# Masked attention: score products in three half banks used in turn, new engine orders, and a later start of the last stage

## The reference, cut to what matters

```
x = x + cross_attention(layernorm(x), ctx)              # 16 heads of 16, with biases
x = x + two_of_eight_experts(layernorm(x))
q, k, v = layernorm(x) Wq, ctx Wk, ctx Wv                # shared 16x16 matrices per head
energy  = where(mask == 0, -1e20, q k^T)                 # the masked attention
x = x + softmax(energy / sqrt(256)) v Wo + bo
x = x + spikes(square(relu(layernorm(x) W_fc)) W_proj)   # the last stage
```

## Time and profile before

| | |
|---|---|
| median of three executions | 3887.06 us (3885.37 to 3891.0) |
| the profiled execution | 3889.76 us, of which the span of the trace is 3888.0 us |
| TensorE busy | 3699.7 us (95%) |
| VectorE busy | 3091.1 us (80%) |
| ScalarE busy | 2208.8 us (57%) |
| GpSimd busy | 2208.9 us (57%) |
| mean granted TensorE clock | 0.979 |

### The profile page before, as it was taken

The page is one execution under the profiler, slowest core; times in us unless marked ns, Lnnn a source line. Parts: engine busy times, 40 slices in busy tenths (PEclk is TensorE's granted clock), DMA queues, the critical chain, the costliest instruction groups (busy, mean ns, idle before and its releaser), DMA issues. The chain is left out here.

```text
span 3888.0 us, 134428 instructions
## 1 busy us (share of the span) xinstructions
PE 3699.7 (95%) x47408; PEld 2875.9 (74%) x47408; DVE 3091.1 (80%) x5266; ACT 2208.8 (57%) x4529; POOL 2208.9 (57%) x3316
## 2 busy tenths in 40 slices
PE   5999999994899999999999996899999989999999
PEld 4777777772677777777777775566666658888888
DVE  4888888886777777777777775799889877777777
ACT  3777777775444444444444442577767764555554
POOL 5666666663354533333333334366656667887777
PEclk9999999997899999999999998899999999999999
DMA  4677777765333322222222223699999962333332
GB/s 123 187 210 206 211 213 219 215 201 160 99 81 80 81 66 74 65 74 65 67 71 65 74 62 87 157 211 212 219 209 209 213 151 80 79 75 76 79 75 72
DMA packets 834241, 502.59 MB, mean 129 GB/s; under 512 B 262037, under 2 KB 824408, under 8 KB 833480
## 3 DMA queue, kind: packets, MB, share of 16 engines
q1 hardware_dynamic: 832680, 493.49, 50.3%
q0 software_dynamic: 928, 0.49, 0.1%
HBM read 251.27 MB, written 214.96 MB: 120 GB/s over the span
## 5 line engine op out<-in xcount | busy, mean ns | idle before, releaser
L1506 ACT ACTIVATE all_region<-phase_loop_hid,phase_b1T 128x128 f32<-128x128 f32 x2048 | 586.1, 368 | 728.0 <-PE phase_loop_hid L193 693.5
L191 PE MATMUL phase_loop_hid<-phase_loop_moe_h,phase_w_hi 128*128 128x128 f16 x4096 | 728.1, 220 | 0.1
L193 PE MATMUL phase_loop_hid<-phase_loop_moe_h,phase_w_lo 128*128 128x128 f16 x4096 | 726.4, 219 | 0.0
L192 PE MATMUL phase_loop_hid<-phase_loop_moe_h,phase_w_hi 128*128 128x128 f16 x4096 | 726.4, 219 | 0.0
L1112 DVE TENSOR_REDUCE phase_loop_mx<-phase_loop_score 128x8 f32<-128x1024 f32 x512 | 625.8, 1222 | 100.6 <-PE phase_loop_score L875 94.8
L1472 PE MATMUL phase_loop_moe_y<-phase_w,all_region 128*128 x2048 | 693.6, 379 | 0.3
L1030 ACT ACTIVATE phase_loop_pt<-phase_loop_scoreT 128x1024 f32<-128x1024 f32 x448 | 458.6, 1024 | 271.5 <-PE phase_loop_scoreT L909 269.2
L1474 PE MATMUL phase_loop_moe_y<-phase_w,all_region 128*128 x2048 | 558.2, 273 | 0.0
L1524 DVE TENSOR_SCALAR all_region<-all_region 128x512 f16<-128x512 f32 x512 | 257.6, 503 | 248.6 <-PE phase_loop_moe_y L1474 192.8
L191 PEld LDWEIGHTS phase_loop_hid<-phase_loop_moe_h,phase_w_hi 128*128 x4096 | 400.6, 98 | 66.5 <-issue 0.4
L1527 DVE SCALAR_TENSOR_TENSOR all_region<-all_region 128x512 f16<-128x512 f32 x512 | 410.1, 801 | 17.6
(11 more groups left out here) (276 smaller groups left out, 9846.6 us busy)
## 6 DMA issues: line engine op xcount, KB each, us to landing
qk_scratch<-phase_loop_qk SPq DMA_DIRECT2D x192, 256.0 KB, 3.5
phase_loop_qS<-qk_scratch SPq DMA_DIRECT2D x768, 64.0 KB, 3.2
phase_loop_cin<-in_ctx SPq DMA_DIRECT2D x128, 256.0 KB, 4.6
x_scratch<-phase_loop_x SPq DMA_DIRECT2D x128, 256.0 KB, 3.1
h_scratch<-phase_loop_hr SPq DMA_DIRECT2D x128, 256.0 KB, 3.8
phase_loop_kS<-qk_scratch SPq DMA_DIRECT2D x384, 64.0 KB, 2.4
ks_scratch<-ct_scratch SPq DMA_DIRECT2D x384, 64.0 KB, 2.4
phase_loop_kS<-ks_scratch SPq DMA_DIRECT2D x128, 192.0 KB, 3.9
```

The source lines that it names most:

```text
L191: eng.matmul(out, l_hi, r_hi, start=start, stop=False)
L192: eng.matmul(out, l_hi, r_lo, start=False, stop=False)
L193: return eng.matmul(out, l_lo, r_hi, start=False, stop=stop)
L1506: i = act.activation(hf[n % NF][:, j, :], hid(u, n)[:, j * S:(j + 1) * S], ACT.Gelu, bias=w["b1"][:, bass.ds(e * HB + (4 * half + j), 1)], ...
```

## The change

Only phase 3 differs.

- The scores go into three half banks in turn: the two of `score` and `ring0`. The eight halves of a unit (n = 0 to 3, hh = 0 and 1) are numbered on through all units, and half number i is in bank i mod 3. The 8 products of `score(n)` are the same; each now writes to the bank of its half.
- `mask_score` handles one half: one matmul of 512 columns, which waits for the half three places before to be read.
- `row_max(n)`, one reduction of 1024 columns, becomes two, `row_max_half(n, 0)` and `row_max_half(n, 1)`, of 512 columns each. The semaphore `s_mx` counts to 8 per unit.
- `o` changes to the ring bank of `t_max`, `q` and `y0`; `t_y` and `y1` share the other one.
- The task lists of all five engines get a new order and, in part, new lags. Nothing else is added or left out.
- `NEXT_START` goes from 5 to 9 (VectorE 6 to 10): the tasks of the last stage join the lists four steps later.

```diff
-NEXT_DEPTH, NEXT_START = 5, dict(zip(("sync", "tensor", "scalar", "gpsimd", "vector"), (5, 5, 5, 5, 6)))
+NEXT_DEPTH, NEXT_START = 5, dict(zip(("sync", "tensor", "scalar", "gpsimd", "vector"), (9, 9, 9, 9, 10)))
...
-        s_s, s_mx, s_st, s_e, s_av = (g(n, NP) for n in "s_s s_mx s_st s_e s_av".split())
+        s_s, s_st, s_e, s_av = (g(n, NP) for n in "s_s s_st s_e s_av".split())
+        s_mx = g("s_mx", NP if first else 2 * NP)
...
-            plan = [(8, "t_y"), (4, "t_max"), (1, "q"), (7, "y1"), (6, "y0"), (8, "o")]
-            shared = ((), ("t_max", "q", "o"), ("t_y", "y1", "y0"))
+            plan = [(9, "o"), (8, "t_y"), (4, "t_max"), (1, "q"), (7, "y1"), (6, "y0")]
+            shared = ((), ("o", "t_max", "q", "y0"), ("t_y", "y1"))
...
+        score3 = half_banks(score_bank) + [ring3[0][:, :]]
+
+        def score_half(u, n, hh):
+
+            return score3[(2 * (NP * u.no + n) + hh) % 3]
...
-                    tasks = [(5, load_c), (1, load_xT), (5, store_max), (3, stack_q), (11, store_x1), (12, store_h),
-                             (2, store_q), (8, load_r), (5, place_max), (2, stack_k)]
+                    tasks = [(5, place_max), (0, load_xT), (2, stack_k), (4, store_max), (2, stack_q), (4, load_c),
+                             (10, store_x1), (11, store_h), (7, load_r), (1, store_q)]
...
-                    tasks = [(11, rows1), (4, maxima), (5, ctx_as_v), (6, cut(p, 3)), (9, rstd1)]
+                    tasks = [(5, ctx_as_v), (9, rstd1), (3, maxima), (10, rows1), (5, cut(p, 3))]
...
-                                m = pe.matmul(score_bank[:, half(hh, j)], qS[u.slot4][rows, b, at], kS[u.slot4][rows, b, at],
+                                to = score_bank[:, half(hh, j)] if first else score_half(u, n, hh)[:, j * S:(j + 1) * S]
+                                m = pe.matmul(to, qS[u.slot4][rows, b, at], kS[u.slot4][rows, b, at],
...
-                def mask_score(n):
+                def mask_score(n, hh):
 
                     def go(u):
-                        s_mx.wait(pe, u, n)
-                        for hh in range(2):
-                            pe.matmul(score_bank[:, hh * 512:(hh + 1) * 512], c["identb"][:, :], w["mask"][:, :], start=True,
-                                      stop=False, skip_group_check=True)
+                        s_mx.wait(pe, u, 2 * n + hh - 2)
+                        pe.matmul(score_half(u, n, hh), c["identb"][:, :], w["mask"][:, :], start=True, stop=False,
+                                  skip_group_check=True)
...
-                    tasks = [(6, av(0)), (3, score(0)), (8, make["t_y"]), (5, mask_score_t(0)), (4, make["t_max"]),
-                             (5, score_t(0)), (3, mask_score(1)), (6, av(1)), (3, score(1)), (5, score_t(1)),
-                             (1, make["q"]), (7, make["y1"]), (3, mask_score(2)), (5, mask_score_t(2)), (3, score(2)),
-                             (6, av(2)), (5, score_t(2)), (6, av(3)), (3, mask_score(3)), (6, make["y0"]),
-                             (3, score(3)), (5, score_t(3)), (8, make["o"]), (2, mask_score(0))]
+                    tasks = [(4, score(3)), (6, score_t(3)), (3, mask_score(0, 0)), (9, make["o"]),
+                             (3, mask_score(0, 1)), (8, make["t_y"]), (6, av(0)), (3, score(0)), (5, mask_score_t(0)),
+                             (3, mask_score(1, 0)), (4, make["t_max"]), (6, av(1)), (5, score_t(0)),
+                             (3, mask_score(1, 1)), (1, make["q"]), (3, score(1)), (5, score_t(1)),
+                             (3, mask_score(2, 0)), (7, make["y1"]), (6, av(2)), (3, mask_score(2, 1)),
+                             (5, mask_score_t(2)), (3, score(2)), (5, score_t(2)), (3, mask_score(3, 0)),
+                             (6, make["y0"]), (3, mask_score(3, 1)), (6, av(3))]
...
-                    tasks = [(5, copy_max), (6, expo(0)), (6, expo(1)), (2, hi_q), (7, copy_y(0)), (6, expo(2)),
-                             (7, copy_y(1)), (10, norm1), (6, expo(3)), (6, expo_under(3)), (8, hi_y)]
+                    tasks = [(8, hi_y), (10, norm1), (4, copy_max), (5, expo(0)), (6, copy_y(0)), (1, hi_q),
+                             (5, expo(1)), (5, expo(2)), (6, copy_y(1)), (5, expo(3)), (5, expo_under(3))]
...
+                def row_max_half(n, hh):
+                    a, g4 = n // 2, n % 2
+
+                    def go(u):
+                        s_s.wait(v, u, n + 1)
+                        if n == 0 and hh == 0:
+                            s_m3.wait(v, u.back(2))
+                        to = mx[u.slot][:, a, :].rearrange("p (h g j) -> p h g j", h=2, g=2)[:, hh, g4, :]
+                        v.tensor_reduce(to, score_half(u, n, hh).rearrange("p (j n) -> p j n", j=CH), AX.X,
+                                        ALU.max).then_inc(s_mx.sem, 1)
+                    return go
...
-                    tasks = [(8, norm_y(0)), (10, add_x), (4, row_max(0)), (10, norm1_stats), (9, lo_y),
-                             (4, row_max(1)), (8, norm_y(1)), (2, lo_q), (4, row_max(2)), (6, cut(v, 1)),
-                             (4, row_max(3))]
+                    tasks = [(4, row_max_half(0, 0)), (9, lo_y), (4, row_max_half(0, 1)), (10, norm1_stats),
+                             (4, row_max_half(1, 0)), (2, lo_q), (4, row_max_half(1, 1)), (8, norm_y(1)),
+                             (4, row_max_half(2, 0)), (4, row_max_half(2, 1)), (7, norm_y(0)),
+                             (4, row_max_half(3, 0)), (4, row_max_half(3, 1)), (6, cut(v, 1)), (9, add_x)]
```

## The result

The changed kernel takes **3932.84 us** (median of 4 executions, 3927.45 to 3934.9) against 3888.39 us for the kernel before in the same session. The ratio is **1.0112, 95% interval 1.0095 to 1.013**: slower by 44 us, outside my range (3873 to 3904). The profiled execution has a span of 3932.0 us, also 44.0 more than the 3888.0 of before.

What follows compares the result with a forecast made beforehand. TensorE was taken as really full at 11.36 us a unit in the steady masked attention. Terms 1 + 4 - 6 + 5.1 = +4.1 us gave 3893.9 on the profiled execution, 3891.2 us as median, range 3873 to 3904.

Steps and rivals of the forecast that it cites:

- loop C: From score(3) through its halves and GpSimd's maxima to t_max: possible at 4.3 us, its place at 4.43, so it fits.
- The new order of waits: Walk through one steady unit's three tight loops: all fit by about 0.1 us; +1 us taken for 57 units.
- TensorE's floor: TensorE's work per steady unit is unchanged by the change and stays 11.36 us.
- VectorE and the halves: Eight half reductions cost VectorE +0.3 us a unit, 10.7 in all, hidden under 11.36; taken as 0.
- second rival: VectorE becomes the bound in the steady units, slower: 3902 to 3914 us, chance 0.12.
- the point of 0.70 us a half: Length of a half reduction from which VectorE's load would decide the steady unit; at 0.75 us, 23 us more.
- The DMA queue: In four steps with large transfers TensorE waits 2.7 us for place_max's rows, plus lower clock: 15.6 for 11.6, +4 us.
- first rival: The waits for place_max's rows vanish as transfers land sooner: 3873.2 us, chance 0.2.
- Fill: Start of phase 3: three banks shorten the mask and reduction loop, t_max comes earlier in the first units; -6 us.
- Drain and later start: End of phase 3: first up product 12.8 us later after a 10.0 us gap, 7.7 regained behind it; +5.1 us.
- steps 66 to 68: Steps of the drain after t_y of unit 58: 28.0 us in the new lists, about as before.
- third rival: The ends cost more, by large transfers holding TensorE or low clock through the drain: +12, 3899 us, chance 0.18.

Runs made afterwards that it cites:

- e1: The changed kernel with VectorE's cut of quarter 1 handling one head's 128 columns in place of all eight: 3909.69 us, ratio 1.0049.
- f6: The kernel before with each row_max split into two half reductions, two banks and all orders as they were: 3885.89 us, ratio 0.9998.
- e3: The changed kernel with t_max behind av(1) in TensorE's list in place of ahead of it: 3933.33 us, ratio 1.0108.
- f4: The kernel before with place_max alone moved, to behind stack_q in the DMA queue's list: 3899.79 us, ratio 1.0025.
- e4: The changed kernel with the last stage beginning two steps earlier (NEXT_START 7 in place of 9): 3925.24 us, ratio 1.0085.
- g2: The kernel before with cut(1) behind row_max(3) in VectorE's list, so that it runs beside GpSimd's maxima: 3916.44 us, ratio 1.0077.
- f1: The changed kernel with place_max behind stack_q in the DMA queue's list, 2.3 us earlier and ahead of the large transfer: 3952.23 us, ratio 1.0163.

## Why the prediction was wrong

**The failed step is loop C of "The new order of waits".** It took the maxima's 2.34 us from a unit in which they run alone, and put t_max possible at 4.3 us against its place at 4.43: "All fit, by about 0.1 us". The new list puts the cut directly behind the last half, beside them. That is 1.06 - 0.29 = 0.77 us more; less the 0.13 of room it is 0.64, and e1 measured 0.66. The rest of the loop came as I had walked it. My +1 us for the loops became +30: the new wait of 0.66 us a unit, less 0.12 that the new list saves (below), 57 times. The page "SBUF — State Buffer" of the Trainium skill (section "Who interferes with whom") has the rule: a VectorE instruction with two inputs in SBUF contends with a GpSimd instruction that reads SBUF, and of the modes in which VectorE takes the whole pair of shared ports it says that whoever issues first has the pair for the whole instruction and the other blocks fully. The traces here agree with the first for this `tensor_tensor`, and nearly with the second: where the cut starts first, L757 ends with it, within 0.15 us; where L444 starts first with 0.61 us still to go, the cut is 0.47 us longer. I had read the earlier trace rows without that question. The kernel before even showed it: its cut takes 1.69 us in the steady part, where GpSimd's L444 (1.16 us) has started first, and 1.22 in its drain, where L444 has not; and in that drain a GpSimd operation of 0.23 us takes 0.80 beside the cut (timelines of GpSimd and VectorE, kernel before):

```profile
3162.52 0.23 POOL L423 TENSOR_SCALAR phase_loop_ln1b_nm<-phase_loop_ln1b_mv 128x2 f32<-128x2 f32 x1
...
3182.83 0.80 POOL L423 TENSOR_SCALAR phase_loop_ln1b_nm<-phase_loop_ln1b_mv 128x2 f32<-128x2 f32 x1
...
3182.32 1.22 DVE L585 TENSOR_TENSOR phase_loop_pt<-phase_loop_pt,all_keep_min 128x1024 f32<-128x1024 f32 x1
```

An earlier start alone does not hold the other up: L412 (`tensor_tensor` of 128x2, 0.73 us) had started at 3182.01, ahead of that cut, and lengthened nothing.

**TensorE's floor.** "The floor stays 11.36 us": e1 shows 11.24 for the new list, so it is 0.12 better (7 us in 57 units), which the wait hid.

**VectorE and the halves: right.** Half 0.69 busy, 0.61 from start to start as in the sum, 0 exposed; f6 confirms it alone. My second rival had the sign right and the cause wrong: VectorE decided, not by its load but by where one operation lies. Its price by the point of 0.70 us a half never applied.

**The DMA queue: right mechanism, mis-sized.** The waits of 2.7 us that I forecast for the large transfers were 3.9, 2.8, 2.6 and 2.2; but the units were 20.2 us too long in place of 15.6, since the issue took 3.5 to 5.4 us where I used 3.1, and the granted clock was 0.93 in that stretch. Elsewhere the longer unit gave the queue room: 3.8 us lost where before had 5.6. Together +6.8 against +4. (Two steps of that sum don't come out as written: 4.4 - 3.1 leaves 1.3 us, not 1.4, and a clock loss of 1.7 us in half of the cases is 0.85 us each, not 1.2. They change it by 1 us.) That this room was only lent shows in e1 and e3. My first rival (the waits vanish with a little more room) fails in f4: the waits for those rows did vanish, and the kernel was slower.

**Fill: -3.1 for -6.** e1 fills in 76.9 us, which is -7.2, so the gain was there and the same contention took part of it; e4, which has the lists of the changed kernel, took 79.0, so about 2 us of this is scatter.

**Drain and later start: +11.0 for +5.1.** The gap was forecast at 10.0 and came at 10.75, the stretch behind the first up product at 682.6 and came at 682.95. What failed is "steps 66 to 68 take 28.0 us, about as before": from t_y of unit 58 to that of unit 61 it is 33.8 us, and from there to the first up 24.7, for which I had 24.9. The steps still pay the cut (1.47 us before t_max at 3205, and ScalarE's exp late behind it). e1 with the same start has 738.0 us for this stretch, so 3.4 of the 11.0 belong to the cut; its three steps take 31.1 us, and why these are still 3 us over my 28.0 stays open. My third rival, the dearer ends, was right in kind for the ends, and small beside the steady part.

## What to carry to other kernels

When a list is reordered, check for each short GpSimd operation on the critical chain which VectorE operation will now run beside it: a `tensor_tensor` with both inputs in SBUF held a 0.3 us operation until its own end here. A duration read from a trace is valid only beside the neighbour that it had there; look for the same operation elsewhere in the trace with another neighbour. And where a second bound stands close behind the first, removing the first gives back only a part: here 25 of 37.6 us (e1).

## What the hardware did that I had not expected

- GpSimd blocked by VectorE: 0.29 to 1.06 us (L757, L751 in g2) beside a cut of 1.22; and VectorE blocked by GpSimd: the cut at 1.69 where L444 (1.16 us) had started 0.55 us ahead of it, 1.22 where only a 128x2 operation had. Reductions and products from PSUM did not do it: the other five maxima operations keep their 0.21 to 0.25 us beside them.
- A large transposing transfer takes its queue for 2.6 to 5.7 us to issue. A small transfer behind it is issued that much later, and TensorE waited up to 3.9 us for it. With a unit of 12.13 us (g2) the same four transfers cost next to nothing.
- Moving a small transfer 2 us earlier cost 20 us, 17.5 of them in the steady part (f1): it had to wait in the queue for the landing of the store it reads.
